# A single-core GNN, linear-attention and mixture-of-experts layer: the start of the first projection reordered, the folded sums stored as rows, the router's sums turned by transposes

## The reference, cut to what matters

```python
xn = _layernorm(x)                                   # x: 1250 x 1024
x = x + gnn(xn, src, dst, W, b) + mix(xn, Wq, bq, Wk, bk, Wv, bv, Wo, bo, P)
x = x + ffn(_layernorm(x), Wg, Wu, Wd, Wr, temperature)

# mix: q, k, v = xn @ Wq.T + bq, ...; k' = relu(k_head @ P_head.T) / 8, q' alike; (k'^T v) per head; @ Wo.T + bo
# gnn: segment sum over 20000 edges and self loops of norm * (xn @ W.T + b)[col]
# ffn: the weights of 8 experts come from the logits
inh = sigmoid(x @ Wr / temperature)
w = exp(-abs(inh - GOLDEN_CENTER) / 0.1) * in_zone   # with a top-2 fallback, then normalised
out = sum_e w_e * (silu(x @ Wg_e) * (x @ Wu_e)) @ Wd_e
```

## Time and profile before

| | |
|---|---|
| median of 3 runs | 1112.64 us (1112.21 to 1113.32) |
| the profiled execution: its own time | 1114.37 us |
| its span | 1112.3 us |
| PE busy | 1088.9 us (98%) |
| DVE, ACT, POOL busy | 373.1, 252.0, 294.7 us |
| mean granted TensorE clock | 0.998 |

### The profile page before, as it was taken

The page is one execution under the profiler, slowest core; times in us unless marked ns, Lnnn a source line. Parts: engine busy times, 40 slices in busy tenths (PEclk is TensorE's granted clock), DMA queues, the critical chain, the costliest instruction groups (busy, mean ns, idle before and its releaser), DMA issues.

```text
span 1112.3 us, 14951 instructions
## 1 busy us (share of the span) xinstructions
PE 1088.9 (98%) x5630; PEld 903.9 (81%) x5630; DVE 373.1 (34%) x993; ACT 252.0 (23%) x397; POOL 294.7 (26%) x246
## 2 busy tenths in 40 slices
PE   5989999999999999999999999999999999999998
PEld 4778778888778888888878888887888888888887
DVE  6664566676641111322212213435321111111111
ACT  4331111111232345311111113334121111112000
POOL 4000011121133246400034554443132233225000
PEclk9999999999999999999999999999999999999999
DMA  6513001222234387604179987874022222216321
GB/s 243 114 30 105 7 19 59 71 61 69 65 122 143 127 299 247 216 1 152 38 218 328 294 243 210 226 208 147 1 86 62 61 61 61 71 52 219 109 98 67
DMA packets 146858, 139.29 MB, mean 125 GB/s; under 512 B 8974, under 2 KB 116834, under 8 KB 146530
## 3 DMA queue, kind: packets, MB, share of 16 engines
q1 hardware_dynamic: 146210, 136.21, 39.7%
q10 hardware_dynamic: 576, 2.10, 0.5%
HBM read 102.32 MB, written 35.96 MB: 124 GB/s over the span
## 4 chain that ended last, share of the span: by engine, by line
PE 95%; DMA 2%; DVE 2%; ACT 1%; issue 0%; SPq 0%; ACTq 0%; DVEq 0%
PE ps L1564 10%; PE ps L1565 9%; PE ps L1566 9%; PE ps L1824 7%; PE ps L1825 7%; PE ps L1826 7%; PE ps L1766 4%; PE ps L1760 4%; PE ps L1740 3%; PE ps L1691 3%; PE ps L1872 3%; PE ps L1741 3%; PE ps L1742 3%; PE ps L1870 3%; PE ps L1692 3%; PE ps L1693 3%
## 5 line engine op out<-in xcount | busy, mean ns | idle before, releaser
L1564 PE MATMUL ps<-w_hi,xnH 128*128 128x512 f32 x480 | 192.5, 401 | 0.0
L1566 PE MATMUL ps<-w_hi,xnL 128*128 128x512 f32 x480 | 188.1, 392 | 0.0
L1565 PE MATMUL ps<-w_lo,xnH 128*128 128x512 f32 x480 | 188.1, 392 | 0.0
L1564 PEld LDWEIGHTS ps<-w_hi,xnH 128*128 128x128 f32 x480 | 91.0, 190 | 19.5
L1566 PEld LDWEIGHTS ps<-w_hi,xnL 128*128 128x128 f32 x480 | 90.8, 189 | 19.6
L1565 PEld LDWEIGHTS ps<-w_lo,xnH 128*128 128x128 f32 x480 | 91.0, 190 | 17.9
L733 POOL TENSOR_TENSOR acc<-acc,cw 128x320 f32<-128x320 f32 x40 | 35.7, 894 | 262.6 <-ACT cw L912 261.5
L1519 DVE TENSOR_TENSOR prd<-ps,wB 128x512 f32<-128x512 f32 (+1 forms) x24 | 14.2, 592 | 162.6 <-PE ps L1826 148.4
L1691 PE MATMUL ps<-xnH,w_hi 128*128 128x512 f32 (+1 forms) x192 | 68.1, 355 | 0.0
L1824 PE MATMUL ps<-x2H,guH 128*128 128x512 f32 (+1 forms) x192 | 67.6, 352 | 0.4 <-ACT wT L1092 0.4
L1825 PE MATMUL ps<-x2L,guH 128*128 128x512 f32 (+1 forms) x192 | 67.6, 352 | 0.0
(11 more groups left out here) (304 smaller groups left out, 2042.1 us busy)
## 6 DMA issues: line engine op xcount, KB each, us to landing
cR<-c_d SPq DMA_DIRECT2D x20, 640.0 KB, 5.1
foldin<-in SPq DMA_DIRECT2D x32, 256.0 KB, 2.8
guR<-in SPq DMA_DIRECT2D x16, 512.0 KB, 5.1
c_d<-cw SPq DMA_DIRECT2D x40, 160.0 KB
w_raw<-in SPq DMA_DIRECT2D x12, 512.0 KB, 6.1
xb<-in SPq DMA_DIRECT2D x10, 512.0 KB, 6.1
qs0H<-qT_d SPq DMA_DIRECT2D x10, 512.0 KB, 5.5
qs0L<-qT_d SPq DMA_DIRECT2D x10, 512.0 KB, 6.8
```

Of the source, the lines that this page charges most:

```text
L1564: pe.matmul(target, xnH[:, kc, cols], wH[w][:, kc, :], start=(kc == 0), stop=False)
L1565: pe.matmul(target, xnH[:, kc, cols], wL[w][:, kc, :], start=False, stop=False)
L1566: mm = pe.matmul(target, xnL[:, kc, cols], wH[w][:, kc, :], start=False, stop=(kc == KC - 1))
```

## The change

**Loads.** x tile 0 is loaded in two halves, the left one first on SP's queue, the right one first on ScalarE's. Behind them stand x tile 1 and panel pieces 1 and 3 on SP's queue, and panel pieces 0 and 2 and x tile 2 on ScalarE's. The semaphore of buffer 0 therefore counts one more landing.

**Tile 0.** ScalarE normalises only its left half, VectorE the right half (xn_right). ScalarE's order of panel copies, tile copies and roots is rewritten, and so is VectorE's order of the first tiles; the edge work of steps 0 and 1 moves to 1 and 2.

**TensorE.** It starts with 26 transposes of the identity (WARM) into bank 7, whose result nobody reads. Row tiles 0 and 1 are then multiplied by products(), in which the terms are ordered by what is ready: for each pair of panel pieces first high x high and low x high, the terms with the panel's low half later, and parts of tile 1 in between.

**The sums.** A transpose (folded_row, step 2) and a ScalarE copy make the folded sums 8 rows of 128 in fbr. SP stores these rows, after x tile 8 and before the fold of kc = 4, and loads kbb after all folds.

**The router.** logits(k) makes ten transposes in three groups, behind expert(0, 0), router(2) and expert(0, 1). VectorE copies the first halves, adds the second halves and divides: three operations for one. ones8 and its GpSimd instructions go.

What is left out below are the allocations of the new tensors and semaphores and GpSimd's counts of constants (each one lower).

```diff
+WARM = 26
...
+        def first_panel(engine, piece):
+            cols = slice(piece * 2 * W, (piece + 1) * 2 * W)
+            engine.dma_start(wR[0][:].rearrange("q k n -> q (k n)")[:, cols], wv_pan[0][:, cols])\
+                .then_inc(in_w[0][piece], 16)
...
+                if t == 3:
+                    sp.wait_ge(xn_right, 1)
                 sp.dma_start(xb[:, t % 3, :], x[t]).then_inc(in_x[t % 3], 16)
...
-            for t in range(3):
-                load_x(t)
+            sp.dma_start(xb[:, 0, 0:W], x[0][:, 0:W]).then_inc(in_x[0], 16)
+            load_x(1)
+            first_panel(sp, 1)
+            first_panel(sp, 3)
...
-            sp.wait_ge(bias_ev, 2)
-            with nc.allow_non_contiguous_dma(reason="1024 sums"):
-                sp.dma_start(fb_d.rearrange("o (c q) -> q (o c)", q=P), bkf[:]).then_inc(fb_st, 16)
-            load_x(6)
-            load_fold(0, 2)
+            for kc in range(2, KC):
+                if kc + 4 < NT:
+                    load_x(kc + 4)
+                if kc == 4:
+                    sp.wait_ge(bias_ev, 3)
+                    sp.dma_start(fb_d.rearrange("o (c q) -> (o c) q", q=P), fbr[:]).then_inc(fb_st, 16)
+                load_fold(0, kc)
             sp.wait_ge(fb_st, 16)
             sp.dma_start(kbb[:], fb_d[:, 0:W].to_broadcast([P, W])).then_inc(in_kb, 16)
...
-
-            for base in (0, -NEXP):
-                pool.affine_select(out=ones8[:], in_=ones8[:], compare_op=ALU.not_equal, fill=1.0, base=base,
-                                   pattern=[[-1, NEXP]], channel_multiplier=1).then_inc(wrs_ok, 1)
-                pool.wait_ge(wrs_ok, 1 if base == 0 else 2)
...
-            for piece in range(4):
-                cols = slice(piece * 2 * W, (piece + 1) * 2 * W)
-                act.dma_start(wR[0][:].rearrange("q k n -> q (k n)")[:, cols], wv_pan[0][:, cols]).then_inc(in_w[0][piece], 16)
+            act.dma_start(xb[:, 0, W:D], x[0][:, W:D]).then_inc(in_x[0], 16)
+            first_panel(act, 0)
+            first_panel(act, 2)
+            act.dma_start(xb[:, 2, :], x[2]).then_inc(in_x[2], 16)
...
+                cols = slice(0, D if t else W)
+                act.activation(xn[:, t % 2, cols], xb[:, t % 3, cols], ACT.Identity, scale=lnw[:, t % 2, 18:19],
                                bias=lnw[:, t % 2, 19:20]).then_inc(xn_done, 1)
 
...
             ln1_sqrt(0)
+            ln1_out(0)
             panel_hi(0, 0, 1)
-            ln1_out(0)
+            x_hi(0, 0)
+            ln1_sqrt(1)
             panel_hi(0, 1, 1)
-            ln1_sqrt(1)
+            x_hi(0, 1)
+            panel_hi(0, 2, 1)
             ln1_out(1)
-            for h in range(2):
-                x_hi(0, h)
-            panel_hi(0, 2, 1)
+            ln1_sqrt(2)
             panel_hi(0, 3, 1)
-            ln1_sqrt(2)
             for h in range(2):
                 x_hi(1, h)
             ln1_out(2)
...
+                if t == 2:
+                    act.wait_ge(bias_mm, 2)
+                    act.activation(fbr[:], bank(5)[0:KC, P:2 * P], ACT.Copy).then_inc(bias_ev, 1)
...
-                dve.wait_ge(in_x[t % 3], 16 * (t // 3 + 1))
+                dve.wait_ge(in_x[t % 3], 16 * (t // 3 + 1) + (16 if t % 3 == 0 else 0))
...
-            def x_low(t):
-                for h in range(2):
+            def x_low(t, halves=range(2)):
...
-            edges = {0: (edges_convert,), 1: (edges_keys,), 3: (edges_reach, lambda: edges_inside(0)),
+            edges = {1: (edges_convert,), 2: (edges_keys,), 3: (edges_reach, lambda: edges_inside(0)),
...
-            for t in range(3):
-                ln1_stats(t)
-                ln1_finish(t)
-                if t >= 1:
-                    x_low(t - 1)
+            ln1_stats(0)
+            ln1_finish(0)
+            dve.wait_ge(ln_step, LN_STEPS)
+            dve.tensor_scalar(xn[:, 0, W:D], xb[:, 0, W:D], lnw[:, 0, 18:19], lnw[:, 0, 19:20], ALU.mult, ALU.add)\
+               .then_inc(xn_right, 1)
+            ln1_stats(1)
+            x_low(0, (0,))
+            ln1_finish(1)
+            x_low(0, (1,))
+            ln1_stats(2)
+            ln1_finish(2)
+            x_low(1)
             ln1_stats(3)
-            for t in range(NT):
+            ln1_finish(3)
+            x_low(2)
+            v_out(0, 0)
+            ln1_stats(4)
+            for t in range(1, NT):
                 if t + 3 < NT:
                     ln1_finish(t + 3)
                 if t + 4 < NT:
...
-            dve.wait_ge(zs_mm, 1)
-            dve.tensor_scalar(zlog[:], bank(7, NT * NEXP), tmp_t[:, 1:2], None, ALU.mult).then_inc(z_step, 1)
+            dve.wait_ge(zs_mm, 3)
+            sums = bank(7, 2 * NT * NEXP).rearrange("q (t k e) -> q t k e", t=NT, k=2)
+            dve.tensor_copy(by_tile(zlog[:]), sums[:, :, 0, :]).then_inc(z_step, 1)
             dve.wait_ge(z_step, 2)
+            dve.tensor_tensor(by_tile(zlog[:]), by_tile(zlog[:]), sums[:, :, 1, :], ALU.add).then_inc(z_step, 1)
+            dve.wait_ge(z_step, 3)
+            dve.tensor_scalar(zlog[:], zlog[:], tmp_t[:, 1:2], None, ALU.mult).then_inc(z_step, 1)
+            dve.wait_ge(z_step, 4)
...
+                    if t == 0 and h == 1:
+                        pe.wait_ge(xn_right, 1)
...
+            def folded_row():
+                pe.wait_ge(bias_ev, 2)
+                pe.transpose(bank(5)[0:KC, P:2 * P], bkf[:], ident[:]).then_inc(bias_mm, 1)
+
...
             def chunk_windows():
                 pe.wait_ge(edge_step, EDGE_MIN)
-                pe.wait_ge(bias_ev, 2)
...
             def range_row():
                 pe.wait_ge(edge_step, EDGE_PAIR)
+                pe.wait_ge(bias_ev, 3)
...
+            def products(t, terms, kcs):
+
+                target, cols = job_bank(("v", 0, t)), slice(t * P, (t + 1) * P)
+                for x_half, w_half in terms:
+                    for kc in kcs:
+                        if w_half == "H":
+                            pe.wait_ge(pan_hi, kc // 2 + 1)
+                        else:
+                            pe.wait_ge(pan_lo, kc // 2 + 1)
+                        if x_half == "h":
+                            pe.wait_ge(xh_done, 2 * t + kc // 4 + 1)
+                        else:
+                            pe.wait_ge(xl_done, 2 * t + kc // 4 + 1)
+                        last = w_half == "L" and kc == KC - 1
+                        mm = pe.matmul(target, (xnH if x_half == "h" else xnL)[:, kc, cols],
+                                       (wH if w_half == "H" else wL)[0][:, kc, :],
+                                       start=((x_half, w_half, kc) == ("h", "H", 0)), stop=last)
+                        if last:
+                            mm.then_inc(mm_done, 1)
+
+
+            for k in range(WARM):
+                pe.transpose(bank(7)[:, 0:P], ident[:], ident[:])
+            transposes(0)
+            for k in range(3):
+                products(0, ("hH", "lH"), (2 * k, 2 * k + 1))
+            transposes(1)
+            products(0, ("hL",), range(0, 4))
+            products(0, ("hH", "lH"), (6, 7))
+            products(1, ("hH",), range(KC))
+            products(0, ("hL",), (4, 5))
+            transposes(2)
+            products(1, ("lH",), range(KC))
+            products(0, ("hL",), (6, 7))
+            products(1, ("hL",), range(KC))
+            for t in range(1, NT):
                 if t in (3, 5, 6):
                     {3: chunk_windows, 5: window_chunks, 6: range_row}[t]()
-                rows(("v", 0, t), t, 0, ready=0 if t == 0 else None)
+                if t >= 2:
+                    rows(("v", 0, t), t, 0)
                 if t + 2 < NT:
                     transposes(t + 2)
                 if t == 1:
                     folded_biases()
+                if t == 2:
+                    folded_row()
                 if 1 <= t <= KC:
                     fold(0, t - 1)
...
-            def logits():
-                pe.wait_ge(z_out, 3)
-                for t in range(NT):
-                    mm = pe.matmul(bank(7)[:, t * NEXP:(t + 1) * NEXP], zTs[:, t * P:(t + 1) * P], ones8[:], start=True,
-                                   stop=True)
+            def logits(k):
+                first, last = ((0, 4), (4, 7), (7, 10))[k]
+                pe.wait_ge(z_out, 2 if k == 0 else k + 1)
+                for t in range(first, last):
+                    mm = pe.transpose(bank(7)[:, 2 * t * NEXP:2 * (t + 1) * NEXP], zTs[:, t * P:(t + 1) * P],
+                                      ident[0:2 * NEXP, 0:2 * NEXP])
                 mm.then_inc(zs_mm, 1)
...
             expert(0, 0)
+            logits(0)
             router(2)
+            logits(1)
             expert(0, 1)
-            logits()
+            logits(2)
```

(19 more changed lines are left out.)

20 lines of the change are left out of this document (7 added, 13 removed).

## The result

The changed kernel takes **1102.03 us** (median of 4 runs, 1101.65 to 1102.08). The kernel before, run beside it on the same chip, takes 1112.98 us (4 runs, three of them those of the table of before; 1112.21 to 1113.77). The ratio is 0.9901, with a 95% interval of 0.9884 to 0.9918. The profiled execution's own time is 1102.07 us for a span of 1100.1, against 1114.37 and 1112.3 before. So the spans of the two profiles differ by 12.2 us and the medians by 10.95. The change is faster, as forecast. In the profiles 12.2 us stand against a sum of 12.0; the median lies 1.4 us above the forecast of 1100.6.

The account below looks back on a forecast made before the run. TensorE, busy 1088.9 of 1112.3 us, was taken as the bound. Gains of 5.5 - 0.7 + 6.4 + 0.8 = 12.0 us from the median 1112.64 gave 1100.6 us, range 1097.5 to 1104.5.

Parts of the forecast that it names:

- Start: Up to tile 3's transposes: they begin at 24.0 instead of 29.53, 5.5 us gained, bounds 3.1 and 7.5.
- 0.7 for the clock: At the start: charge, out of 0 to 2.4 us, for TensorE's clock perhaps not being raised or not staying up.
- signs of being wrong: Matmul pace of 0.43 beyond 17, panel pieces landing later than 7.5, 10, 10 and 12.6, or new TensorE idle after 85.
- the first rival: At the start: the clock stays low until about 17.5 us, costing 1.7 us more, time 1102.3; chance 0.2.
- Middle: Between tile 3's transposes and row tile 9: stops and low clock behind the store go, 6.4 us gained, bounds 2.9 and 7.0.
- the wait for cx: TensorE's 2.74 us stop before 61.22, for VectorE's cx: 0.3 us stay and 2.4 go.
- The clock's term: Behind the stop before 61.22: the clock stays up, giving 1.1 us, half of 2.2 at 0.51.
- The second rival: In the middle: VectorE takes the place of the late x, the cx stop and its clock remain, 1104.5; chance 0.12.
- Router: Logits: 2.2 us of records become ten transposes and three gaps, 0.8 us gained, bounds 0 and 1.1.
- Nothing absorbed later: Rival, after the middle: kbb or edge work absorbs the gain, leaving 1107 to 1112; chance 0.05.
- no fall of the clock in the long part: Rival, long part: the granted clock falls; 1.1% below full eats the 12.0 us, 2% gives 1122; chance 0.03.
- What would show it: Expected marks, among them tile 0's transposes at 8.6, tile 3's at 24, row tile 9's addition at 85, logits 1.4 us.

Follow-up runs that it names:

- the new store alone: The kernel before with only the store of the sums (transpose into eight rows, copy) and SP's order changed: 1107.01 us, ratio 0.9932.
- the router's experiment: The kernel before with only the router's logits changed to ten transposes in three groups and three VectorE operations: 1112.14 us, ratio 0.9985.
- x tile 0 whole: The changed kernel with the first loads of before, x tiles 0 to 2 whole on SP's queue and four panel pieces on ScalarE's: 1103.47 us.
- the version with the edge columns first: The changed kernel with the four operations of edges_inside(1) moved ahead of VectorE's statistics in step 4: 1100.77 us, ratio 0.9884.

## Why the prediction was right, point by point

- **Start: 5.5, less 0.7 for the clock, so 4.8.** Measured 29.53 - 24.61 = 4.9. Its parts were less exact, and that they add up is luck. x was there at 4.56 for 4.8, but ScalarE's half tile took 0.81 us for 0.65, and panel piece 1 landed at 10.84 where I had 10.0. That is one of my signs of being wrong, panel pieces later than 7.5, 10, 10 and 12.6: they landed at 7.1, 10.8, 10.2 and 13.1. TensorE lost 2.3 us behind its first own transposes where I had 1.7 (24.61 - 8.61 - 13.7). These 0.6 us took the place of the 0.7 I had charged for the clock, which was high from the first own transpose on and cost nothing. VectorE's half took 0.55 us, near the middle of its bounds, and lay beside ScalarE's.
- **The clock.** The rule of the Trainium skill, "TensorE: Matmul & The Clock Gate", part on the PE-mode transpose, did not hold here, for f32 transposes: eight own transposes take 1.09 us with 26 transposes before them and 1.94 without. The start without them is worth 29.53 - 25.39 = 4.1 us, where I had 3.1 at a low clock: the level rose by 14.9 and not at 17.5. So the first rival's price was too high by a microsecond even if its condition had come true. Its time, 1102.3, is close to the median measured; it is the rows that speak against it, not the time.
- **Middle: 6.4.** Measured 11.2 - 4.9 = 6.3. The stop near 46 is gone, the clock stays up, and 0.78 us of the wait for cx stay instead of 0.3, so this term was 0.4 too large. The clock's term, 1.1, was 0.4 too small: I took the 2.2 us of the window in the earlier trace rows for the whole stretch, and it is 2.94 us of work, worth half of that, 1.5. The two errors cancel, which is luck again. The window in the kernel before:

```profile
61.22:64.16 2.94, 2.94 (x9) 2.32 (x10) 2.87 (x7) 0.00 (x0) 0.00 (x0) 0.50 0.03 6
```

  The cause of the late x is right in its place, the store, and half right in its way: tile 6 stood behind no wait for the landing, its transfer was slow. The second rival (1104.5) had the right place, as the chain shows VectorE from 23.00 to 51.35, but not the size: the arrears of VectorE came mostly from the late x, as the forecast said. In the new store alone TensorE has no wait for cx at all; with the quicker start it has 0.78 us.
- **Router: 0.8.** Measured 1.0, the upper end of 1.1 nearly reached.
- **Nothing absorbed later, no fall of the clock in the long part.** kbb, issued at 67.40, appears in no wait of TensorE, and from 86.05 to 765 us TensorE's busy time in each window equals that of before. Row tile 9 came at 86.05 where "What would show it" has 85; the sum itself gives 97.25 - 4.8 - 6.4 = 86.05, so the 85 was a slip.
- **Against the median.** I took the 12.0 us from the median of 1112.64 and had 1100.6; the median is 1102.03, 1.4 more. The sum was made in a profiled execution that stood 1.7 us above that median, and the scatter of about 1 us in the first stage, which the router's experiment shows, is part of what the change took away: the changed kernel's medians are 1102.03 and 1101.78, while those of the kernel before lie between 1112.98 and 1114.27. By medians the gain was 10.95 us in the first comparison and 12.5 in the last. The term that was missing fits this: in the shorter executions of before there is less of a stop to remove. The profile of the router alone is such a one, with 67.10 us in the second column of the table for 67.72.
- **What the sum did not say** is that its first two terms hang together. Each was costed with the other part in place, which is why the sum held. The start by itself, costed in the same way, would have been put at 4.8 us, and 0.7 to 1.7 would have come.

## What to carry to other kernels

When two waits stand one behind the other on the same path, cost the removal of the first both with the second in place and with it gone; the head start gained ahead of a fixed arrival is simply waited away, and work that was moved behind that arrival then delays what follows. A transfer of many single elements delays the transfers issued right behind it too, so look at their time to landing and not only at who waits for the store. When a wait is shortened and not removed, read the chain ahead of it: if it is one engine's without a gap, reorder that engine's queue by who is waited for first. Small operations that someone waits for go ahead of long ones whose result is due a step later.

## What was not expected of the hardware

- **Transposes alone raised TensorE's clock.** It rose at a different moment in each profiled execution, though nothing ahead of them differs: 26 of them took between 4.37 and 5.81 us. In the changed kernel's profile, with 5.81, all 26 still ran at the slow pace, 0.21 us from one to the next, and the trace's clock record has the rise at 7.96, in the gap of 0.95 us behind them.
- **Whether it falls back behind them does not go by the length of the idle gap alone.** With 3.00 us of idle time (x tile 0 whole) it was still high when the own transposes began and fell 0.3 us later. With 2.04 us (old router) it fell during them, at 9.2, so that eight took 1.65 us. After 2.56 us in the version with the edge columns first they took 1.09 us and the matmuls stayed fast; after 1.24 us in the changed kernel, as measured again, the first matmuls were slow. No run here settles what decides it.
- **The clock fell with TensorE busy all the time.** In the profiled execution of the new store alone it did so behind the 20 small logits matmuls (16 rows, 8 columns each) of the old router. Its timeline and windows:

```profile
782.97 2.39 PE L1804 MATMUL ps<-ones,zTs 16*128 16x8 f32 x20
787.34 0.63 PE L1831 MATMUL ps<-x2H,guH 128*128 128x512 f32 x1
782.00:788.00 6.00, 6.00 (x33) 5.03 (x32) 1.95 (x7) 0.27 (x1) 1.98 (x3) 0.84 0.01 3
788.00:790.00 2.00, 2.00 (x7) 1.52 (x7) 1.55 (x10) 0.43 (x2) 0.00 (x0) 0.62 0.01 4
```

  A matmul takes 0.63 us there instead of 0.39, without any idle time. The granted clock is 0.50 from 786.1 to 789.5. That execution has a span of 1106.5 against 1104.8 to 1105.2 of its three neighbours, some 1.5 us, and behind row tile 9 it has 1.7 us more than the two other profiles with the old router (1016.8 for 1015.1). The two groups of the changed kernel with the old router lie 1.8 us apart, which would fit the same event; its long executions were not profiled, so this is argued and not shown. In the profile of before the clock did not fall there, and the router alone, with the new transposes, has two executions that are 1.5 to 2 us longer than its other eight. So whether the new router ever saves more than its 1.0 us is open.
